# One packed word of tile counts for TensorE, and eight experts written out

## The reference

```python
h = _layernorm(x) * (1 + ca) + sa
x = x + ga * attn(h, ...)            # conv, silu, selective scan, output projection
h = _layernorm(x) * (1 + cb) + sb
x = x + gb * ffn(h, ...)
...
# ffn: E = 8, TOPK = 2, I = 938
out = swiglu(x, shared_gate_up, shared_down)
probs = softmax(x @ gate_weight.T)
top_p, sel = top_k(probs, 2)         # normalised to a sum of 1
for e in range(E):
    out = out + cw[..., e:e+1] * swiglu(x, experts_gate_up[e], experts_down[e])
```

## Time and profile before

| | |
|---|---|
| runs | 809.44, 813.05, 813.42 us, median 813.05 |
| profiled execution | 809.22 us, of which the span of instructions 807.4 us |
| granted TensorE clock, mean | 0.919 of full |
| PE / PEld busy | 689.7 us (85%) / 530.3 us (66%) |
| DVE / ACT / POOL busy | 571.8 us / 427.3 us / 368.6 us |
| routed experts | about 416 to 770 us of the span, 19 tiles |

### The profile page before, as it was taken

How to read it: one execution, slowest core, us unless ns; L and a number is a source line. 1 busy time by engine, 2 the same in 40 slices (tenths; PEclk the granted TensorE clock), 3 DMA queues, 4 the chain that set the end, 5 groups by cost and what they waited for, 6 DMA issues and landing times.

```text
span 807.4 us, 11914 instructions
## 1 busy us (share of the span) xinstructions
PE 689.7 (85%) x3134; PEld 530.3 (66%) x3135; DVE 571.8 (71%) x1230; ACT 427.3 (53%) x822; POOL 368.6 (46%) x300
## 2 busy tenths in 40 slices
PE   4769988988898898887779998999989999999910
PEld 1556766666676666666558777877777787787710
DVE  4867979879887888987636665666656666666637
ACT  4457465575747558453435554555555555555510
POOL 1404554537355453727237281828145163822136
PEclk9577999899999989998989999999999999999965
DMA  8202000000000000000310403123003103110036
GB/s 261 73 1 92 27 18 23 13 26 26 26 26 26 17 10 29 24 26 28 98 61 1 125 19 117 40 89 116 26 14 120 43 3 111 39 33 23 28 122 199
DMA packets 38202, 44.37 MB, mean 55 GB/s; under 512 B 5334, under 2 KB 28880, under 8 KB 38184
## 3 DMA queue, kind: packets, MB, share of 16 engines
q1 hardware_dynamic: 33576, 35.69, 14.4%
q0 software_dynamic: 4608, 8.47, 3.2%
HBM read 31.42 MB, written 13.76 MB: 56 GB/s over the span
## 4 chain that ended last, share of the span: by engine, by line
PE 60%; DVE 21%; issue 7%; ACT 4%; POOL 3%; DMA 2%; SPq 1%; DVEq 1%; POOLq 0%; ACTq 0%
PE PS L587 56%; PE PS L590 4%; DVE acc L1226 2%; DVE delta L1247 1%; DVE X L1327 1%; DVE prod L1208 1%; DVE wd L1299 1%; DVE r L1375 1%; ACT L1033 1%; DVE oh L1378 1%; POOL w_lo L416 1%; DMA xin<-sorted_dram 1%; DVE stats_a L1193 1%; DVE nx_b L1325 1%; POOL w_hi L411 1%
## 5 line engine op out<-in xcount | busy, mean ns | idle before, releaser
L928 ACT ACTIVATE sg<-PS 128x512 f32<-128x512 f32 x216 | 129.4, 599 | 213.9 <-PE PS L587 213.1
L1208 DVE TENSOR_TENSOR PS<-PS,sg 128x512 f32<-128x512 f32 x160 | 111.8, 699 | 133.3 <-PE PS L587 133.3
L587 PE MATMUL PS<-xh,w_lo 128*128 128x512 f32 x432 | 188.4, 436 | 19.8 <-issue 11.4
L587 PE MATMUL PS<-xl,w_hi 128*128 128x512 f32 x432 | 173.0, 400 | 0.0
L587 PE MATMUL PS<-xh,w_hi 128*128 128x512 f32 x432 | 172.8, 400 | 0.0
L546 POOL DMA_INDIRECT result_dram<-y_rows,aux_d x80 | 78.1, 976 | 197.2 <-DVE y_rows L1578 161.8
L587 PEld LDWEIGHTS PS<-xh,w_lo 128*128 128x128 f32 x432 | 83.7, 194 | 50.1 <-issue 20.6
L481 POOL DMA_INDIRECT sorted_dram<-h,slot x64 | 71.5, 1118 | 92.4 <-DVE slot L1413 65.9
L1213 DVE TENSOR_TENSOR al<-PS,ah 128x512 fp32r<-128x512 f32 x160 | 109.1, 682 | 1.4
L935 ACT CAST ah<-PS 128x512 fp32r<-128x512 f32 x160 | 93.1, 582 | 7.7 <-DVE PS L1208 7.7
L587 PEld LDWEIGHTS PS<-xl,w_hi 128*128 128x128 f32 x432 | 83.6, 194 | 18.8
(11 more groups left out here) (222 smaller groups left out, 1127.4 us busy)
## 6 DMA issues: line engine op xcount, KB each, us to landing
stage<-in_w_gu SPq DMA_DIRECT2D x18, 469.0 KB
xin<-sorted_dram SPq DMA_DIRECT2D x20, 260.0 KB, 2.7
stage<-in_w_dn SPq DMA_DIRECT2D x9, 448.0 KB
tab<-mods_dram SPq DMA_DIRECT2D x8, 384.0 KB, 3.4
sorted_dram<-pad SPq DMA_DIRECT2D x8, 260.0 KB, 2.4
out<-X SPq DMA_DIRECT2D x4, 512.0 KB, 3.2
stage<-result_dram SPq DMA_DIRECT2D x3, 512.0 KB, 5.1
result_dram<-y_rows,aux_d POOLq DMA_INDIRECT x80, 2.2
```

What stands on the lines that cost most here:

```text
L587: return nc.tensor.matmul(out, lhsT, rhs, start=start, stop=stop, **k)
L928: A.activation(sg[:, c % 3, :], bank("gate", where, c), ACT.Silu).then_inc(s["silu_done"], 1)
L1208: V.tensor_tensor(product_in(where, c), bank("up", where, c), sg[:, c % 3, :], ALU.mult).then_inc(s["prod_done"], 1)
```

## The change

DVE gets three more small operations behind the plan: (tiles - 1) of each expert times 8 to the power of the expert's number, the sum over the experts, and a copy of that sum to an int32 word, announced by a semaphore `word_ready`. TensorE waits for it once, loads the word once, and moves it into a named register. For every expert it takes the low three bits, adds 1, copies the count and the running number of tiles into values of their own, and after the expert's tiles adds the count to the running number and shifts the word right by three bits. The eight experts are written out, so TensorE's program holds eight copies of `tile_body`. The wait for the weights is against a constant. A constant row `digit` of eight columns is added to `small`.

```diff
--- before.py
+++ after.py
@@ -58,6 +58,7 @@
 ROW = P + 2
 NOWHERE = 4 * TOKENS
 SHARED = TOKENS // TILE
+MAX_TILES = TOKENS // TILE
 EPS = 1e-5
 
 CONST = ("ident", "below7", "above7", "lvl6", "lvl5", "lvl4", "later16", "upto16", "before", "ones")
@@ -89,7 +90,8 @@
     expert = np.arange(E)[None, :] + 0 * u
     seg = np.tile(np.arange(GC) > 0, E)[None, :] & (u >= 0)
     many = np.arange(E)[None, :] * TILE + 0 * u
-    small = np.concatenate([upto, equal, block, *roles, seg, E - expert, expert * REGION, many], 1)
+    digit = MAX_TILES ** np.arange(E)[None, :] + 0 * u
+    small = np.concatenate([upto, equal, block, *roles, seg, E - expert, expert * REGION, many, digit], 1)
     big = np.concatenate([np.broadcast_to(m, (P, P)) for m in mats], 1)
     token = (np.arange(CH)[None, :, None] * P + np.arange(P)[:, None, None]) * 2 + np.arange(2)[None, None, :]
     return (np.ascontiguousarray(big, np.float32), np.ascontiguousarray(small, np.float32),
@@ -99,7 +101,7 @@
 SMALL = {}
 _at = 0
 for _name, _n in (("upto", BLK), ("equal", BLK), ("block", NB), ("upper", 9), ("lower", 9), ("seg", E * GC),
-                  ("rev", E), ("region", E), ("many", E)):
+                  ("rev", E), ("region", E), ("many", E), ("digit", E)):
     SMALL[_name] = (_at, _n)
     _at += _n
 NSMALL = _at
@@ -202,6 +204,8 @@
         plan_f = sb("plan_f", [P, 4, E])
         plan = sb("plan", [P, 3, E], I32)
         cmp = sb("cmp", [P, E, E])
+        word_f = sb("word_f", [P, 1])
+        word = sb("word", [P, 1], I32)
         pad = sb("pad", [P, TR, ROW])
 
         xh = sb("xh", [P, TILE], F32R)
@@ -255,7 +259,7 @@
             xh_ready xl_ready logits_done lg_ready soft_in soft_out picked_ready counts_done counts_read
             rows_ready sorted_out dve_chain raw_in split_hi split_done  piece_hi piece_done gate_done up_done silu_done prod_done
             ah_ready al_ready al_late down_done y_bank_done y_sb_ready yt_done y_out gated_free tile_in xt_done rh_ready
-            rl_ready aux_read aux_moved results_out plan_ready pads_out final_added final_gated final_sum final_ready_dve final_ready_pool
+            rl_ready aux_read aux_moved results_out plan_ready word_ready pads_out final_added final_gated final_sum final_ready_dve final_ready_pool
             out_done gb_in""".split()
         names += [f"final_in{g}" for g in range(G)]
         s = {n: sem("s_" + n) for n in names}
@@ -272,7 +276,6 @@
         NFIRST = 3
         EARLY = 14
         NRAW = 4
-        MAX_TILES = TOKENS // TILE
         MAX_FIRST = 2 * TOKENS // TILE + E
 
         def tile_count(engine, e):
@@ -898,20 +901,26 @@
                 down(buf, I, FC - 2, WIDE)
                 down(buf, I, FC - 1, WIDE)
 
-            def expert(e, buf, first=None):
-                if first is None:
-                    tiles, first = tiles_of(pe, e)
-                else:
-                    tiles = tile_count(pe, e)
+            pe.wait_ge(s["word_ready"], 1)
+            digits = pe.value_load(word[0:1, 0:1], min_val=0, max_val=MAX_TILES ** E - 1)
+            bits = MAX_TILES.bit_length() - 1
+            left = pe.alloc_register("tiles_left")
+            here = pe.alloc_register("tiles_here")
+            done = pe.alloc_register("tiles_done")
+            pe.reg_mov(left, digits)
+            pe.reg_mov(done, 0)
+            for e in range(E):
+                pe.reg_alu(here, left, MAX_TILES - 1, ALU.bitwise_and)
+                pe.reg_add(here, here, 1)
+                tiles = pe.snap(here, min_val=1, max_val=MAX_TILES)
+                first = pe.snap(done, min_val=0, max_val=MAX_FIRST)
                 pe.wait_ge(s["split_done"], e + 2)
                 apart(pe)
                 with pe.Fori(0, tiles) as t:
-                    tile_body(buf, first + t)
-                return first + tiles
-
-            with pe.Fori(0, E // 2 - 1) as k:
-                expert(2 * k + 1, 0, expert(2 * k, 1))
-            count = expert(E - 1, 0, expert(E - 2, 1))
+                    tile_body((e + 1) % 2, first + t)
+                pe.reg_add(done, done, here)
+                pe.reg_alu(left, left, bits, ALU.logical_shift_right)
+            count = pe.snap(done, min_val=1, max_val=MAX_FIRST)
             pe.wait_ge(s["rl_ready"], count + 1)
             turn_result(SHARED + count - 1, WIDE)
 
@@ -1556,6 +1565,9 @@
             V.tensor_copy(plan[:, 2, :], base[:])
             V.tensor_copy(plan[:, 0:2, :], plan_f[:, 0:2, :]).then_inc(s["plan_ready"], 1)
             V.engine_nop().then_inc(s["aux_read"], 1)
+            link(V.scalar_tensor_tensor(plan_f[:, 3, :], plan_f[:, 0, :], -1.0, S["digit"], ALU.add, ALU.mult))
+            link(V.tensor_reduce(word_f[:], plan_f[:, 3, :], AX.X, ALU.add))
+            V.tensor_copy(word[:], word_f[:]).then_inc(s["word_ready"], 1)
             product(g, 1, WIDE)
             for c in range(1, FC):
                 if c + 1 < FC:
```

## The result

The changed kernel takes 799.47 us, median of four runs (799.35 to 801.30), against 811.25 us, median of four runs of the kernel before (807.41 to 813.42). The ratio is 0.9879, 95% interval 0.9844 to 0.9915. Taken again beside the experiments on another chip it was 0.9893 (0.9840 to 0.9947). So the gain is 9 to 12 us by the medians, and 4 to 13 us by the two intervals. The forecast was 805.0 us and faster, within 799.5 to 810.5. The measured median lies at the lower bound of that range (0.03 us under it), where the forecast had put the case that all of the cost at the beginnings is hidden. The two profiled executions are 809.22 and 799.48 us, 9.74 apart.

The account below looks back on a forecast made before the run. TensorE was taken to set the pace, with 11.4 us of waits mostly at the experts' beginnings. Gains 5.7 + 0.3 + 1.6 - 0.1 = 7.5 us gave 805.0 us, range 799.5 to 810.5.

Parts of the forecast that it names:

- The loads: TensorE, beginnings of experts 1 to 7: ten loads, address arithmetic and outer loop go, 8.9 us gained; 0.71 us a load.
- The unpacking: TensorE, each expert's beginning: six new register operations cost 0.45 us, 3.2 us over seven, leaving 5.7 us gained.
- the price by the operation: Register work at a beginning: 0.20 us for about four address operations gives 0.30 us for six; by the instruction 0.60.
- Expert 0: Beginning of expert 0: 0.6 us earlier by one load and two addresses less, counted as 0.3 us gained.
- The plan: DVE's three operations delay TensorE up to 0.6 us; slack of 0.59 before the first routed turn leaves 0.1 us cost.
- a rival that the clock falls there: Behind the plan, 0.55 us more idle drops TensorE's clock: cost 2.2 us instead of 0.1, 807 us; chance 0.06.
- The clock: Expert 2: the fall to 1.2 GHz behind the 2.11 us wait no longer happens, 1.6 us gained.
- All hidden: Beginnings of experts: register work runs ahead and no wait is left, 11.7 us gained, 800.5 us; chance 0.13.
- The dear unpacking: Beginnings stay near 0.82 us because unpacking costs as much as the load; gain 3.3 to 4.7, 809.0 us; chance 0.18.
- Code loading: TensorE's longer program stalls on instruction fetches at branches and first entries, 18 x 1.31 = 24 us, 829 us; chance 0.05.
- Next in line: ACT after a shorter beginning: silu may be 0.3 us late, but is ready before the first down projection; cost 0.
- The level: Starting time for the sum: median 813.05 gives 805.5 us, mean of four 811.3 gives 803.8; 805.0 was predicted.

Follow-up runs that it names:

- the doubled work: The changed kernel with a second set of named registers, four register operations more for each expert: 802.41 us, ratio 0.9905 to the kernel before.
- straight code alone: The kernel before with its eight experts written out and nothing else, twelve loads kept at fixed addresses, no packed word: 803.46 us, ratio 0.9930.
- counts loaded in the tile: The kernel before, experts written out, next expert's count loaded mid tile, no packed word, none of DVE's three operations: 800.25 us, ratio 0.9871.
- the three operations alone: The kernel before with DVE's three operations for the word added, TensorE not reading it and keeping its loads and outer loop: 809.37 us, ratio 1.0014.
- the pair of experiments: The changed kernel with six unused loads more: three each at experts 2 and 4 (808.89 us), or one each at experts 1 to 6 (805.82 us).
- the packed-word kernel with its loop: The changed kernel with its six first experts again in a loop of three passes, four tile bodies and not eight: 800.25 us, ratio 0.9902.

## Why the prediction was right, and where it was not

**What bounds.** Right: TensorE, and 11.4 us of waits at the beginnings. All of the gain that the two traces show lies there and in the clock.

**The loads.** Right in kind and size: 0.71 us a load with its check, read from differences, and 0.71 us in the experiment that adds one. The sum over ten loads stands. As for the Trainium skill's floor of about 600 ns for `tensor_load` (DMA: Bandwidth & Descriptors, Latency and other measured facts): the 0.71 us is above it and includes the check of bounds, so it does not contradict the page; no run here parts load and check.

**The unpacking.** The term was too large. I took 0.45 us a beginning; 0.42 is left in all, of which 0.11 was there without it, so it is 0.31. That is 1.1 us over seven beginnings: 6.8 gained and not 5.7. The figure is that of the price by the operation (0.30 for six), but the doubled work speaks against this reading: four operations cost 0.33 us, 0.08 each, so six would cost 0.5, more than the whole wait. With 0.08 for the and, the adds and the shift and nothing for the two copies both runs come out: 0.33 of the 0.42 us, and 0.42 - 2 x 0.08 = 0.26 where four operations leave a beginning and two moves come (0.21 to 0.25 measured). So the price is nearer to the one by the instruction (0.10), with the copies free. That the copies are free is inferred; no run prices them.

**Where it shows, and why.** I left open whether a load waits for an empty engine or the sequencer is held at the matmul that waits for DVE. The load in the middle of the tiles settles the first: it does not. Held at the waiting matmul fits all runs: the same load costs 0 in mid tile and 0.71 us behind the last `al_ready`. The changed kernel's timeline bears it out: DVE's last low part is ready at 452.74 + 1.44 = 454.18, 0.10 us before the matmul that takes it starts, while that of chunk 5 was ready 0.9 us ahead (451.38 for 452.31). It isn't shown directly, since no trace has a record of the sequencer. And a rival stands: every load at a beginning is also behind the end of the inner loop, and no run puts one behind the last matmul but inside the loop. That the loop's end, and not the waiting matmul, is what exposes the load is therefore not excluded.

**Expert 0.** 0.3 us forecast, and 0.93 us later measured, with 2.4 us gained by the clock in that execution. The step failed: the first routed turn was released by the gating and not by the rows. The low clock behind the plan brought that about, not the 0.5 us of DVE's operations: in the trace with a load in mid tile, where the clock held there, the rows released the turn as forecast (414.09), and in the traces without these operations but with a low clock (straight code alone, counts loaded in the tile) the gating did. The clock there was low in most profiles of the kernels with a word (full in three of eleven), so the 2.4 us are no steady gain.

**The plan.** 0.1 us was forecast, with "0.6 without the cover" and a rival that the clock falls there (0.06). In the profiled execution the rival happened: TensorE was idle 3.01 us, the clock fell at 404 us, the shared result was turned 416.02 - 413.90 = 2.1 us later. It did not cost 2.2 us, since expert 0 started only 0.93 later and at full clock. Over runs its cost isn't measurable: 1.0014 (0.9984 to 1.0045) for the three operations alone. The chance was too low all the same: the clock was low behind the plan in 11 of the 13 profiles of the changed kernel and the experiments, also in the two without DVE's operations (straight code alone, and counts loaded in the tile), and not in that of the earlier trace rows. It held behind idle times of 2.54, 3.02 and 2.53 us and fell behind others of 2.5 and 3.0. What decides it is open.

**The clock.** Right in place and price: 1.6 us a fall, and 2.9 us for two in the pair of experiments. How often it falls isn't settled. The kernel before has two waits of 2.1 us; behind them its trace shows one fall and that of DVE's operations alone none, with 2.4 us both fell.

**The sum, mended.** Beginnings 6.8, clock 1.6, expert 0 -0.9 to +0.3 with the plan in it, rows 0 to -0.5: 7.0 to 8.7 us. Measured are 11.8 us between the first medians (7 to 13 by the interval) and 8.8 us on the other chip (4 to 13). The larger first difference holds what runs of one kernel differ by (808.97, 810.56 and 811.25 for the kernel before) and perhaps a second fall; what part each has is open. The sum of the forecast, 7.5 us, lies inside the mended range, partly by luck: the cost of the unpacking was put 1.1 us too high, the gain at expert 0 up to 1.1 too high, and the longer waits for rows at nothing.

**The rivals.** All hidden (800.5 us) came nearest in time, but not by its mechanism: the beginnings do not reach 0, as the trace shows. The lower end of the range was set for this rival, so that the measured time met it is luck. The dear unpacking is out. Code loading as a cost of the change is out: fetches of the whole span rose,

```profile
q8 instruction: 11, 0.18, 0.1%
```

from 8 in the kernel before and in the packed-word kernel with its loop, and no beginning waits more for it. But the forecast's argument against the Trainium skill's rule of two blocks and a stall at each branch outside them (Runtime: NRT & Kernel Launch, Instruction fetch mechanics) does not hold. The two tile bodies of the outer loop are 320 matmuls and weight loads, more than one block of 256 and fewer than two; the window of the earlier trace rows has 1190 matmuls and 1190 weight loads in six passes, some 400 a pass. Register instructions, which no view counts, come on top. Counted so, no loop here is shown to leave a window of two blocks, so no trace here tests the rule.

**Next in line.** ACT is ready in time: its first silu of expert 7 still starts 1.19 us after its last copy, and no down projection waits. In the timeline of ACT:

```profile
726.24 0.60 ACT L937 ACTIVATE sg<-PS 128x512 f32<-128x512 f32 x1 [1.19 <-PE PS L590]
```

TensorE began at 724.86, and by the forecast's 1.0 us wanted it from 725.9 on; it came 0.3 to 0.4 us late, as forecast, and no wait of TensorE follows. What I left out is SP's rows: with the beginnings short, PE waits 0.25 to 0.9 us for them in several executions. They are the next wait to look at.

**The level.** The forecast of 805.0 sat near the 805.5 that the sum gives from the median of 813.05. That median was high: the kernel before was at 808.97 to 811.25 in the result and the three sets beside the experiments. From the mean of 811.3, which I had too, the same sum gives 803.8, and with 6.8 for 5.7 at the beginnings 802.7. So 1.2 us of the miss of 5.5 is the level (805.0 - 803.8), 1.1 the price of the unpacking, and of the rest no single term is shown to be the cause; the other chip's median, 801.78, is 3.2 us from the forecast.

## What to carry to other kernels

Price a load or register operation by where it stands, not by itself: between the last matmul of one loop and the first of the next it costs its full time (0.71 and 0.08 us here), in the middle of the loop body it showed no cost. Read such prices from pairs of places that differ by one instruction, start to start, since the modelled ends hide 0.2 us. And look for the longest idle pieces first: here one of over 2 us cost a stretch at half clock besides in some cases (1.4 to 1.6 us, behind one of four pieces of 2.1 us and both of 2.4).

## What the runs showed of the hardware that was not expected

Two idle pieces of 2.4 us cost some 3 us more than the same idle time in small pieces, as TensorE's granted clock went from 2.4 to 1.2 GHz behind each; behind pieces of 1.53 us and less it stayed at 2.4 from expert 1 to 750 us in all kernels, and behind four of 2.1 us it fell once. That is no rule for other places: at expert 0, where several waits of 0.8 to 1.8 us follow each other, it was low in 11 of the 14 profiles. Nineteen register loads in the middle of TensorE's tiles cost nothing that a trace or a time shows. With four tile bodies more in TensorE's program the core drew eleven instruction fetches instead of eight, and no wait of TensorE grew by it.
